# Diagonal 32x32 blocks and compact states in a gated linear recurrence

## What is computed

```python
def step(S, inp):                     # S: [b, 16, 32, 32], in order of the 1024 tokens
    qt, kt, vt, gt = inp
    S = S * jnp.exp(gt)[..., None] + kt[..., None] * vt[..., None, :]
    yt = jnp.einsum('bhk,bhkv->bhv', qt, S)
    return (S, yt)
q = (x @ Wq.T).reshape(b, l, H, K) * K ** (-0.5)
k = (x @ Wk.T).reshape(b, l, H, K)
v = (x @ Wv.T).reshape(b, l, H, V)
g = jax.nn.log_sigmoid(x @ Wg.T).reshape(b, l, H, K)
y, final_state = _gla_recurrence(q, k, v, g)
o = _layernorm(y.reshape(b, l, d), gamma, beta) @ Wo.T
```

## Time and profile before

| | us |
|---|---|
| median of three runs | 2700.03 |
| lowest, highest | 2691.61, 2712.86 |
| the profiled execution | 2717.68 |
| its span | 2715.9 |
| in it, the first recurrence | about 0 to 445 |
| TensorE busy over the span | 2276.5 (84%) |

### The profile page before, as it was taken

How to read it: one execution, slowest core, us unless ns; L and a number is a source line. 1 busy time by engine, 2 the same in 40 slices (tenths; PEclk the granted TensorE clock), 3 DMA queues, 4 the chain that set the end, 5 groups by cost and what they waited for, 6 DMA issues and landing times. The chain is left out here.

```text
span 2715.9 us, 50355 instructions
## 1 busy us (share of the span) xinstructions
PE 2276.5 (84%) x19076; PEld 1967.0 (72%) x19076; DVE 1591.6 (59%) x3469; ACT 1073.6 (40%) x2039; POOL 1032.8 (38%) x809
## 2 busy tenths in 40 slices
PE   8999993789887599996669995999999999999930
PEld 6888882667665488885446773899999899999930
DVE  4555554444453386866985642656665566655657
ACT  3222222345554132322442111555555555555523
POOL 3454451121221100001530276656666666656621
PEclk9999996798897696877899997999999999999965
DMA  2110102144433654552431001233344624233147
GB/s 105 36 36 24 36 28 101 68 160 163 157 147 143 184 155 106 157 104 81 155 122 70 1 1 55 84 135 108 107 143 164 215 89 140 80 129 135 40 174 274
DMA packets 154518, 299.74 MB, mean 110 GB/s; under 512 B 66841, under 2 KB 93209, under 8 KB 139645
## 3 DMA queue, kind: packets, MB, share of 16 engines
q1 hardware_dynamic: 108285, 181.82, 20.8%
q0 software_dynamic: 44480, 115.41, 12.6%
q10 hardware_dynamic: 1616, 0.62, 0.1%
HBM read 296.83 MB, written 106.27 MB: 148 GB/s over the span
## 5 line engine op out<-in xcount | busy, mean ns | idle before, releaser
L91 PE MATMUL bank<-routed_xh,routed_guh 128*128 128x256 f32 (+1 forms) x1536 | 438.0, 285 | 27.8 <-DVE routed_xl L2130 27.8
L92 PE MATMUL bank<-routed_xh,routed_gul 128*128 128x256 f32 (+1 forms) x1536 | 437.9, 285 | 0.0
L93 PE MATMUL bank<-routed_xl,routed_guh 128*128 128x256 f32 (+1 forms) x1536 | 435.9, 284 | 0.0
L2164 DVE TENSOR_TENSOR routed_gul<-routed_guf,routed_guh 128x2816 fp32r<-128x2816 f32 x64 | 198.0, 3093 | 250.8 <-ACT routed_guh L2107 250.8
L91 PEld LDWEIGHTS bank<-routed_xh,routed_guh 128*128 128x128 f32 (+1 forms) x1536 | 281.4, 183 | 35.4 <-issue 32.9
L2048 POOL DMA_INDIRECT routed_x<-mid_x,routed_xi x132 | 277.5, 2102 | 55.1 <-issue 52.6
L93 PEld LDWEIGHTS bank<-routed_xl,routed_guh 128*128 128x128 f32 (+1 forms) x1536 | 282.7, 184 | 0.0
L92 PEld LDWEIGHTS bank<-routed_xh,routed_gul 128*128 128x128 f32 (+1 forms) x1536 | 280.8, 183 | 2.1
L2057 POOL DMA_INDIRECT mid_y<-routed_y,routed_yi x132 | 138.8, 1052 | 246.5 <-ACT routed_y L2123 223.9
L2107 ACT CAST routed_guh<-routed_guf 128x2816 fp32r<-128x2816 f32 x64 | 163.5, 2554 | 34.2 <-DMA routed_guf<-in_GU,routed_wi 29.6
L2117 ACT CAST routed_ih<-routed_sil 128x256 fp32r<-128x256 f32 (+1 forms) x192 | 78.0, 406 | 241.4 <-DVE routed_sil L2169 241.4
(11 more groups left out here) (455 smaller groups left out, 5999.5 us busy)
## 6 DMA issues: line engine op xcount, KB each, us to landing
last_y<-mid_y SPq DMA_DIRECT2D x16, 1536.0 KB, 9.7
mid_ks<-ffn_kT SPq DMA_DIRECT2D x16, 1024.0 KB
mid_qs<-ffn_qT SPq DMA_DIRECT2D x16, 1024.0 KB
ttt_KQ<-mid_ks SPq DMA_DIRECT2D x16, 1024.0 KB, 6.7
ttt_KQ<-mid_qs SPq DMA_DIRECT2D x16, 1024.0 KB, 12.4
mid_te<-ffn_te SPq DMA_DIRECT2D x16, 264.0 KB
ttt_te<-mid_te SPq DMA_DIRECT2D x64, 66.0 KB, 5.8
gla_xT<-in_xT SPq DMA_DIRECT2D x16, 256.0 KB, 3.0
```

What stands on the lines that cost most here:

```text
L91: pe.matmul(out, hi(c), whi(c), start=start and c == 0, stop=False, skip_group_check=True)
L92: pe.matmul(out, lo(c), whi(c), start=False, stop=False, skip_group_check=True)
L93: last = pe.matmul(out, hi(c), wlo(c), start=False, stop=stop and c == n - 1, skip_group_check=True)
L2164: nc.vector.tensor_tensor(gul[q][:].rearrange("p a c n -> p (a c n)"), guf[q][:], guh[q][:].bitcast(F32).rearrange("p a c n -> p (a c n)") ...
```

## The change

L573, L592 and L601 compute only the diagonal blocks: each of their 16 matmuls becomes four of 32x32 weights and 32 columns moved, ordered so that four that follow one another lie on different row groups and different column groups of the array. kvm, Sh and carry keep only the blocks of a head with itself (128 columns for 512), so the mask `heads` goes, and causal is 128x32. The states move from GpSimd to VectorE, in the place of its key_values, with the sum taken straight from PSUM. ScalarE spreads Sh into Shx, full 128x128 blocks with zeros, by the mask `own` (four activations of 512 columns), behind turned(n); L606 reads Shx. beta_all gets a memset of its own.

```diff
@@ gpsimd
+            nc.gpsimd.memset(beta_all[:], 0.0).then_inc(s["zeroed"], 1)
...
             for n in range(N):
-                states(n)
                 with_shift(n)
@@ scalar
+            def widened(n):
+                act.wait_ge(s["Sh"], (NSUB + 1) * n + NSUB)
...
+                    act.wait_ge(s["y"], n)
+                for j in range(HG):
+                    last = nc.scalar.activation(Shx[:, :, :, j], Sh[:], ACT.Copy, scale=own[:, j:j + 1])
+                last.then_inc(s["Shx"], 1)
...
                     turned(n)
+                    widened(n)
@@ vector
-            def key_values(n):
+            def states(n):
+                def scaled(out, in_, c):
+                    nc.vector.tensor_tensor(out, in_, decay[:, :, c:c + 1].to_broadcast([P, KC, DH]), ALU.mult).then_inc(s["Sh"], 1)
+                first = (NSUB + 1) * n
+                dve.wait_ge(s["decay"], n + 1)
...
+                    dve.wait_ge(s["Shx"], n)
+                    dve.wait_ge(s["Sh"], first)
+                scaled(Sh[:, 0], carry[n % 2][:], 0)
                 dve.wait_ge(s["kv"], n + 1)
                 for c in range(NSUB):
-                    nc.vector.tensor_tensor(kvm[:, c], BK[c][:].rearrange(chunks, c=KC),
-                                            heads[:].unsqueeze(1).to_broadcast([P, KC, P]), ALU.mult).then_inc(s["kvm"], 1)
+                    dve.wait_ge(s["Sh"], first + c + 1)
+                    nc.vector.tensor_tensor(kvm[:, c], BK[c][:, 0:KC * DH].rearrange(chunks, c=KC), Sh[:, c], ALU.add).then_inc(s["kvm"], 1)
+                    dve.wait_ge(s["kvm"], NSUB * n + c + 1)
+                    scaled(Sh[:, c + 1] if c < NSUB - 1 else carry[n % 2][:], kvm[:, c], c + 1)
...
-                    nc.vector.tensor_tensor(Am[:, j], BK[j][:].rearrange(chunks, c=KC),
-                                            causal[:].unsqueeze(1).to_broadcast([P, KC, P]), ALU.mult).then_inc(s["Am"], 1)
+                    nc.vector.tensor_tensor(Am[:, j], BK[j][:, 0:KC * SUB].rearrange(chunks, c=KC),
+                                            causal[:].unsqueeze(1).to_broadcast([P, KC, SUB]), ALU.mult).then_inc(s["Am"], 1)
@@ tensor, key_values
-                    for c in range(NSUB):
-                        last = pe.matmul(BK[c][:, m * P:(m + 1) * P], Kr[c * SUB:(c + 1) * SUB, m * P:(m + 1) * P],
-                                         V[n % 2][c * SUB:(c + 1) * SUB, m * P:(m + 1) * P], start=True, stop=True, skip_group_check=True)
+                    for turn_ in range(NSUB):
+                        for j in range(HG):
+                            c, h = (j + turn_) % NSUB, slice((m * HG + j) * DH, (m * HG + j + 1) * DH)
+                            last = pe.matmul(BK[c][j * DH:(j + 1) * DH, m * DH:(m + 1) * DH], Kr[c * SUB:(c + 1) * SUB, h],
+                                             V[n % 2][c * SUB:(c + 1) * SUB, h], start=True, stop=True, skip_group_check=True)
@@ tensor, scores
-                    for j in range(HG):
-                        last = pe.matmul(BK[j][:, m * P:(m + 1) * P], KT[j * DH:(j + 1) * DH, m, :], QT[j * DH:(j + 1) * DH, m, :],
-                                         start=True, stop=True, skip_group_check=True)
+                    for turn_ in range(NSUB):
+                        for j in range(HG):
+                            t = slice((j + turn_) % NSUB * SUB, ((j + turn_) % NSUB + 1) * SUB)
+                            last = pe.matmul(BK[j][t, m * SUB:(m + 1) * SUB], KT[j * DH:(j + 1) * DH, m, t], QT[j * DH:(j + 1) * DH, m, t],
+                                             start=True, stop=True, skip_group_check=True)
@@ tensor, outputs
-                        pe.matmul(Y[:, h * DH:(h + 1) * DH], Am[:, j, m, :], V[n % 2][:, h * DH:(h + 1) * DH],
-                                  start=(k == 0 and m == 0), stop=False, skip_group_check=True)
-                pe.wait_ge(s["Sh"], (NSUB + 1) * n + NSUB)
+                        for c in range(NSUB):
+                            t = slice(c * SUB, (c + 1) * SUB)
+                            pe.matmul(Y[t, h * DH:(h + 1) * DH], Am[t, j, m, :], V[n % 2][t, h * DH:(h + 1) * DH],
+                                      start=(k == 0 and m == 0), stop=False, skip_group_check=True)
+                pe.wait_ge(s["Shx"], n + 1)
```

More of the change, by code:

```diff
@@ L238, in gated_recurrence @@
     ident, cum, sel = ph.sb("ident", [P, P]), ph.sb("cum", [P, P]), ph.sb("sel", [P, NSUB + 1])
-    causal, heads = ph.sb("causal", [P, P]), ph.sb("heads", [P, P])
+    causal = ph.sb("causal", [P, SUB])
     gamma, beta = ph.sb("gamma", [P, KC]), ph.sb("beta", [P, KC])
@@ L246, in gated_recurrence @@
     QT, KT = ph.sb("QT", [P, KC, P]), ph.sb("KT", [P, KC, P])
-    Am, kvm, Sh = ph.sb("Am", [P, HG, KC, P]), ph.sb("kvm", [P, NSUB, KC, P]), ph.sb("Sh", [P, NSUB, KC, P])
-    carry, decay = ph.sb2("carry", [P, KC, P]), ph.sb("decay", [P, KC, NSUB + 1])
+    Am, kvm, Sh = ph.sb("Am", [P, HG, KC, SUB]), ph.sb("kvm", [P, NSUB, KC, DH]), ph.sb("Sh", [P, NSUB, KC, DH])
+    Shx, own = ph.sb("Shx", [P, NSUB, KC, HG, DH]), ph.sb("own", [P, HG])
+    carry, decay = ph.sb2("carry", [P, KC, DH]), ph.sb("decay", [P, KC, NSUB + 1])
     yn, yTh, yTl = ph.sb("yn", [P, D]), ph.sb("yTh", [P, KC, P], F32R), ph.sb("yTl", [P, KC, P], F32R)
@@ L292, in _ @@
             for t, src in ((cum, K["cum"]), (sel, K["sel"]), (gamma, a["gamma"]), (beta, a["beta"]),
-                           (ident, K["ident"]), (causal, K["causal"]), (heads, K["heads"])):
+                           (ident, K["ident"]), (causal, K["causal"]), (own, K["own"])):
                 sp.dma_start(t[:], src).then_inc(s["consts"], 16)
@@ L533, in _ @@
                 if n < N:
-                    key_values(n)
+                    states(n)
                 if n:
@@ L600, in outputs @@
                         h = m * HG + j
-                        pe.matmul(Y[:, h * DH:(h + 1) * DH], Am[:, j, m, :], V[n % 2][:, h * DH:(h + 1) * DH],
-                                  start=(k == 0 and m == 0), stop=False, skip_group_check=True)
-                pe.wait_ge(s["Sh"], (NSUB + 1) * n + NSUB)
+                        for c in range(NSUB):
[3 more added lines that the diff above has]
+                pe.wait_ge(s["Shx"], n + 1)
                 for m in range(KC):
                     for c in range(NSUB):
-                        last = pe.matmul(Y[c * SUB:(c + 1) * SUB, m * P:(m + 1) * P], QT[:, m, c * SUB:(c + 1) * SUB], Sh[:, c, m, :],
+                        last = pe.matmul(Y[c * SUB:(c + 1) * SUB, m * P:(m + 1) * P], QT[:, m, c * SUB:(c + 1) * SUB], Shx[:, c, m].rearrange("p j d -> p (j d)"),
                                          start=False, stop=(m == KC - 1), skip_group_check=True)
@@ L2313, in shape_constants @@
         "sel": sel,
-        "causal": same & (src <= dst),
+        "causal": tok[:, None] % SUB <= np.arange(SUB)[None, :],
         "tri": ((tok[:, None] // TTT) % HG == tok[None, :HG * TTT] // TTT) & (tok[:, None] % TTT <= tok[None, :HG * TTT] % TTT),
@@ L2330, in shape_constants @@
         "free": np.stack(np.broadcast_arrays(0, NOWHERE + np.arange(TILES * SLOTS)), 1),
-        "heads": (tok[:, None] // DH) == (tok[None, :] // DH),
     }
```

13 lines of the change are left out of this document (8 added, 5 removed), and 2 rows, old and new, of the table s.

## The result

The changed kernel takes 2676.74 us (median of 20 runs, 2656.32 to 2696.61) where the kernel before, run beside it, takes 2701.9 us (20 runs, 2691.58 to 2730.06). The ratio is 0.9898 with a 95% interval of 0.9873 to 0.9923: 1.0% faster, about 27 us (25 between the medians; the ratio leaves out two executions of the changed kernel that were over 1.5% above its fastest). The forecast was 1.6%, 42 us. The time lies inside the stated range of 2638 to 2765 us and just above the 2675 where the likeliest case's own range ended: the direction holds, the size falls short by a third.

The account below looks back on a forecast made before the run. TensorE's blocks were taken to bound the first recurrence: -31.9 us in fifteen tiles, -35.5 with the last, -6 for the clock, so 2717.7 gives 2676 us profiled; against 2700.0 timed, 2658 us (-1.6%), range 2638 to 2765.

Parts of the forecast that it names:

- likeliest case: Whole kernel: the forecast of shorter blocks and half the clock loss given back; own range 2638 to 2675 us, chance 0.50.
- What bounds the stage: First recurrence: time is the sum of TensorE's blocks; what VectorE or GpSimd save is worth nothing by itself.
- The three blocks: Key-values, scores, scores times V: each 1.22 us, so +0.12, +0.11 and -2.36 us, -2.13 us a tile.
- rival 1: Three new blocks: instruction stream sets the pace, 27.5 ns a pass, +76 us, 2776 us; chance 0.26 above 19.5 ns, 0.06 between.
- Tile 0: One of fifteen tiles of the first recurrence that were each to gain 2.13 us, together -31.9 us.
- Clock: TensorE's clock falls behind scores times V: half of the 13 us loss given back, -6 us; bounds all or as much again lost.
- Last tile: Last tile of the first recurrence, scores times V 5.64 us partly at half clock: total saving goes from -31.9 to -35.5 us.
- VectorE, ScalarE, GpSimd at nothing: Edits on these engines in each tile cost nothing; 7 us of slack ahead of L606, 43 us if that cover were gone.
- Rival 2: Scores times V: four row groups take turns on one PSUM bank, block 4.1 us, +12 us, 2712 us; chance 0.09.
- Rival 3: States, chained over PE, VectorE and ScalarE, come late for L606 or hold lead_x; full price 43 us, 2743 us; chance 0.03.
- Rival 4: Clock falls oftener: 13 us lost instead of 6 gained, -22 us in all, 2678 us; chance 0.06.

Follow-up runs that it names:

- later transfers: One wait moves the transfers of x by 2 us, in the changed kernel (2746.3 us, ratio 0.989 to the kernel before) and in Products only (2713.56 us, ratio 0.9779).
- Products only: Kernel before with only the product of scores and V cut into diagonal 32x32 blocks: 2666.23 us, ratio 0.9867; on another chip 2715.8 us, ratio 0.9833.

## Why the prediction was right and where it was wrong

- **What bounds the stage** was right: the sum of TensorE's blocks. (The rows of "issue" in the earlier trace rows are those of the weight loads; TensorE's matmuls waited for nothing there.) POOL's work fell by 174.6 us and ScalarE's rose by 40, and neither shows; another 36 us on ScalarE don't either.
- **The three blocks** were right in size, 1.22, 1.21 and 1.22 us for a forecast of 1.22, and a tile of 22.25 for 22.3. The reason given was not. I derived 32 ns for a group of four passes from a rate per column, side by side only on disjoint rows and columns (the rate, 0.87 to 0.9 ns for 32 columns, gives 28 to 29; 32 was the top of the span). By that rule four matmuls that share rows or columns go one after the other and the block takes 4.1 us: it takes 1.22. On one part of the array it takes 2.67 instead of 4.1, and with half the columns moved 1.15. What is seen inside a block is another picture: the first 32 passes of key-values and scores go off within 0.2 us, those of the products within 0.3, and the rest follow at 8.3 ns each. Twenty-one ns a pass on one part would be 5.2 ns with four side by side, so something else sets the 8.3; that it is the supply of instructions to the array was argued, not shown. That 32 ns for four and 8.3 for one come to one block length is luck.
- **The term that failed is one that the sum didn't have: stops for instructions.** The prediction had the stream as rival 1, but as a pace: a price for each pass, equal in all blocks, with a point of decision at 15 ns. It's not a pace but a reserve. 128 passes come at 8.3 ns from what has been fetched, and beyond 256 instructions in some 3.4 us TensorE stops. That long runs go at 27 to 31 ns, near the upper bound of 27.5 that I took from the earlier trace rows, is a coincidence: the 16 passes of that row are 32 instructions, far from 256. The row that should have given the term was in the earlier trace rows together: 422 instructions of TensorE a tile with 23 packets become 998, 3.9 packets of 256 in 22.3 us, and 320 of the 998 (the products and L617) fall into 2.2 us. It cost 6.5 us of idle time in tiles 1 to 14, some 8.7 with what the records of passes cover.
- **Tile 0** was to gain 2.1 us and lost 1.2. It holds the 1.94 us stop shown above, and behind it the clock is at half (mean 0.50 from 40 to 44 us), so that Wq takes 5.12 us from 40.76 to 45.88 instead of 2.9.
- **Clock.** Forecast -6, half of what the lower clock cost before: the 354.7 us are 12.7 more than 14 x 24.43, with the granted clock at 0.50 for 27 us of them. The busy time says -5.9, but 2.2 us of what is left belongs to the stops, so the clock's part is some -8 (12.7 to 4.7). That either is near the forecast is chance, since the same kernel has some 10, 0 and 17 us at half clock in these tiles in its three profiled executions. In this one the low tile, 26.70 us at 0.82, begins right behind the 2.26 us stop at 166.3. With that stop at 1.12 us (later transfers) the tile kept its clock, but so it did behind a stop of 2.5 us in the second run of the same kernel; the runs don't settle when a stop brings the fall. Products only has 0 and 3 us at half clock there.
- **Last tile**: -5.5 for -3.6 (the 35.5 less 31.9 for the other fifteen tiles), but not as forecast. The -3.6 was -4.0 for the products and +0.4 for the other two blocks, and the -4.0 took 64 ns for a group of four passes at half clock, twice the 32. No run shows such a group at 64 ns; with the granted clock at 0.50 four of the second 65 passes of this block take some 54 ns. The products take 3.60 us for 5.64, -2.0 instead of -4.0, because a stop for instructions of 1.82 us stands in them; key-values 1.46 for 2.02 and less time at half clock around them do the rest.
- **VectorE, ScalarE, GpSimd at nothing** was right. The states take 0.292 us each, 0.33 apart, as forecast, and ACT waits for them 0.3 us a tile:

```profile
227.65 0.29 DVE L485 TENSOR_TENSOR gla_kvm<-bank,gla_Sh 128x128 f32<-128x128 f32 x1 [0.68 <-PE bank L580]
227.98 0.29 DVE L472 TENSOR_TENSOR gla_Sh<-gla_kvm,gla_decay 128x128 f32<-128x128 f32 x1
...
229.60 2.57 ACT L396 ACTIVATE gla_Shx<-gla_Sh,gla_own 128x512 f32<-128x512 f32 x4 [0.29 <-DVE gla_Sh L472]
```

  They end at 232.2 and L617 starts at 239.60: 7.4 us of slack, for 7 forecast.
- **Rival 2** (one bank for four row groups) is out: the products are as long as the others. **Rival 3** (the chain comes late) is out by the doubled spread. **Rival 4** (the clock falls oftener) didn't come.

In the stage, then, forecast -41.5 and measured -34.1, 7.4 apart: +6.5 for stops and +3.3 for tile 0, less 1.9 in the last tile, are +7.9; the blocks gained 0.7 more than their forecast. (With the stops at 8.7 and the clock at -8 instead of -6 the sum is the same.)

**The better kernel** is the smallest edit: cut only the block that loaded 128 columns of weights for 32 moved. It's 1.3% and 1.7% faster than before in two timings, where the whole change is 0.9% to 1.1% in four (one of them with the later transfers); with the later transfers it was 2.2%, of which a good part is in stages that the edit doesn't touch. Key-values and scores were at 1.10 us before, with 32 passes; cut fine they cost 0.1 us more and four times the instructions.

## What to carry to other kernels

Cut a block fine only where it gets shorter by it; where it doesn't, it only spends instructions. When an edit multiplies the instructions of TensorE, count them per stretch of a few microseconds and not per tile: here 256 in much less than 3.4 us could mean a stop, of up to 2.8 us, with "issue" as its name and its place in the middle of a block as its sign. And when a number agrees, change the size that it was derived from once: here the length was right and the law behind it wrong.

## What the runs showed of the hardware that was not expected

- Passes of f32 with 32x32 weights follow one another at 8.3 ns at full clock when neighbouring matmuls differ in rows or columns of the array, with 16 or 32 columns moved; at 20.9 ns when eight in a row use the same part. With the granted clock at 0.50 the second half of the last tile's products (65 passes) takes 1.04 us, 13 ns a pass inside it.
- TensorE's instructions arrive in packets of 256 (16384 bytes): 998 a tile with 54 packets in fourteen tiles, where 422 a tile had 23. One that comes late makes a stop of up to 2.8 us, which ends 2.2 to 3.0 us after the packet's start. Two starts were never under 3.26 us apart in any run, and long runs of short passes go at 27 to 31 ns a pass.
- Where 256 instructions follow 256 without slack (three times the scores), a packet starts 0.8 to 1.7 us after TensorE has begun the 256 before.
- The kernel's transfers can hold a packet up: moving those by 2 us moved its start at one place from 166.09 to 165.06 us, out of the span of the other executions. At the other places that isn't shown, nor why stops come and go there from run to run.
